# A mixture-of-experts layer: expert results added to the resident rows by transfers instead of by engines

## What is computed

```python
x = x + tanh(g_xattn) * xattn(layernorm(x), ctx, ...)        # 32 sequences of 64 rows
xf = layernorm(x)
probs = softmax(xf @ gate_w.T); top_p, top_i = top_k(probs, 2)        # 8 experts
y = sum over the two chosen experts e of
    p_e * (silu(xf @ fc1[e].T) * (xf @ fc2[e].T)) @ proj[e].T         # width 176
shared = silu(xf @ s1.T) * (xf @ s2.T) @ shared_proj.T                # width 704
y = y + sigmoid(xf @ shared_gate_w.T) * shared
x = x + tanh(g_ffn) * y
```

## Time and profile before

| | |
|---|---|
| median of 3 runs | 327.76 us (327.75 to 328.55) |
| the profiled execution | 328.36 us |
| its span | 326.6 us |
| mean granted TensorE clock | 0.969 |
| TensorE busy | 285.0 us, 87% |
| VectorE busy | 219.9 us, 67% |
| ScalarE busy | 170.6 us, 52% |
| GpSimd busy | 116.4 us, 36% |

### The profile page before, as it was taken

How to read it: one execution, slowest core, us unless ns; L and a number is a source line. 1 busy time by engine, 2 the same in 40 slices (tenths; PEclk the granted TensorE clock), 3 DMA queues, 4 the chain that set the end, 5 groups by cost and what they waited for, 6 DMA issues and landing times.

```text
span 326.6 us, 5834 instructions
## 1 busy us (share of the span) xinstructions
PE 285.0 (87%) x1783; PEld 252.2 (77%) x1783; DVE 219.9 (67%) x694; ACT 170.6 (52%) x399; POOL 116.4 (36%) x146
## 2 busy tenths in 40 slices
PE   0696979989998987797899999899999999999962
PEld 0565959878877765486788887789999999998852
DVE  3655766969868773666466764787777777743684
ACT  1537677777655454355023554456666666644220
POOL 0510351441773416641450000014444444441840
PEclk9999999999999998699799999999999999999985
DMA  6460114211044102533242565344666644314935
GB/s 225 171 194 0 67 49 130 64 48 66 36 135 163 51 19 99 189 136 101 107 151 65 198 206 188 113 134 137 202 203 202 201 139 135 109 67 138 350 125 193
DMA packets 25999, 43.32 MB, mean 133 GB/s; under 512 B 2961, under 2 KB 19601, under 8 KB 25969
## 3 DMA queue, kind: packets, MB, share of 16 engines
q1 hardware_dynamic: 22128, 33.20, 31.8%
q0 software_dynamic: 3408, 9.57, 8.1%
q10 hardware_dynamic: 432, 0.18, 0.3%
HBM read 26.35 MB, written 16.59 MB: 131 GB/s over the span
## 4 chain that ended last, share of the span: by engine, by line
PE 57%; DVE 20%; ACT 10%; issue 6%; DMA 4%; POOL 1%; SPq 0%; DVEq 0%; ACTq 0%; POOLq 0%
PE bank L416 43%; PE bank L639 8%; DVE ew_lo L961 4%; ACT ew_hi L741 4%; PE bank L716 3%; PE bank L681 2%; DVE work L1260 2%; DMA weight_stage<-wa_dram 2%; DVE xt_lo L961 2%; ACT sh_hi L741 2%; DVE neg_max L1001 2%; DMA weight_stage<-ew_dram 1%; ACT xn_all L778 1%; DVE sh_lo L961 1%; ACT work L773 1%
## 5 line engine op out<-in xcount | busy, mean ns | idle before, releaser
L1420 POOL DMA_INDIRECT y_d<-work,dest_of_slot x39 | 37.4, 959 | 88.4 <-ACT work L741 87.2
L416 PE MATMUL bank<-ew_hi,xt_hi 128*128 (+2 forms) x172 | 58.2, 339 | 0.3 <-issue 0.3
L416 PE MATMUL bank<-ew_lo,xt_hi 128*128 (+2 forms) x172 | 51.8, 301 | 0.0
L416 PE MATMUL bank<-ew_hi 128*128 128x256 f32 (+1 forms) x100 | 33.1, 331 | 15.8 <-ACT ew_hi L741 14.1
L961 DVE TENSOR_TENSOR xt_lo<-bank,xt_hi 128x256 fp32r<-128x256 f32 (+2 forms) x90 | 35.7, 398 | 11.6 <-ACT xt_hi L741 11.5
L416 PE MATMUL bank<-ew_hi,xt_lo 128*128 (+1 forms) x133 | 40.6, 305 | 0.0
L416 PE MATMUL bank<-xt_hi,sw_hi 128*128 128x512 f32 x88 | 36.1, 410 | 2.0 <-DVE work L1260 2.0
L741 ACT ACTIVATE xt_hi<-bank 128x256 fp32r<-128x256 f32 (+1 forms) x90 | 36.3, 409 | 2.8 <-PE bank L424 1.6
L416 PE MATMUL bank<-xt_lo,sw_hi 128*128 128x512 f32 x88 | 35.6, 405 | 0.0
L961 DVE TENSOR_TENSOR ew_lo<-bank,ew_hi 128x512 fp32r<-128x512 f32 (+1 forms) x41 | 22.7, 581 | 19.0 <-ACT ew_hi L741 18.9
L416 PE MATMUL bank<-xt_hi,sw_lo 128*128 128x512 f32 x88 | 35.3, 401 | 0.0
(11 more groups left out here) (157 smaller groups left out, 705.6 us busy)
## 6 DMA issues: line engine op xcount, KB each, us to landing
work<-xs_d SPq DMA_DIRECT2D x39, 136.0 KB, 2.5
weight_stage<-ew_dram SPq DMA_DIRECT2D x10, 486.5 KB, 4.2
ew_hi<-y_d SPq DMA_DIRECT2D x8, 512.0 KB, 7.9
xn_all<-x_dram SPq DMA_DIRECT2D x4, 512.0 KB, 5.0
work<-ctx_t_dram SPq DMA_DIRECT2D x4, 512.0 KB, 3.4
x_d<-work SPq DMA_DIRECT2D x4, 512.0 KB, 2.9
work<-x_d SPq DMA_DIRECT2D x3, 512.0 KB, 3.3
z_d<-work SPq DMA_DIRECT2D x3, 512.0 KB, 3.5
```

Source lines behind the costliest of these rows:

```text
L416: last = nc.tensor.matmul(dst, a, b, start=(n == 0), stop=(n == len(pairs) - 1))
L1420: nc.gpsimd.indirect_dma_start(out=y2_d, out_offset=bass.IndirectOffsetOnAxis(ap=IX[:, n:n + 1], axis=0), in_=EY[:, n % 4, :], in_offset=N ...
```

## The change

SyncE no longer loads the expert results, and the buffer `Y2`, GpSimd's four additions and VectorE's four (`combine`, with the semaphores `g_c1` and `v_c2`) are gone. GpSimd waits for the scatters and issues eight transfers of 512 KB from `y2_d` that add to `XNR`: first those of choice 0 for chunks 3, 0, 1, 2, each after the chunk's partial sums are loaded, then those of choice 1, each after the one of choice 0 for its chunk has landed. `s_sums(LAST)` and the stores wait for the transfers of choice 1.

```diff
@@ SyncE
-            sp.wait_ge(e_y, SLOT_TILES)
-            for r in range(4):
-                sp.wait_ge(d_ey[r], 16 * len(range(r, SLOT_TILES, 4)))
-            for c in LAST_FIRST:
-                for i in range(TOP):
-                    sp.dma_start(Y2[i][:, c * TPC:(c + 1) * TPC, :], y2_t[i, c]).then_inc(d_y[i][c], 16)
             for c in range(LAST - 1):
-                sp.wait_ge(v_c2, c + 2)
+                sp.wait_ge(d_y[1][c], 16)
                 sp.dma_start(out_c[c], XNR[:, c * TPC:(c + 1) * TPC, :]).then_inc(d_out, 16)
             for t in range(LAST * TPC, N_T):
                 sp.wait_ge(v_z, t + 1)
                 sp.dma_start(out_t[t], XNR[:, t, :]).then_inc(d_out, 16)
-            sp.wait_ge(v_c2, N_CH)
+            sp.wait_ge(d_y[1][LAST - 1], 16)
             sp.dma_start(out_c[LAST - 1], XNR[:, (LAST - 1) * TPC:LAST * TPC, :]).then_inc(d_out, 16)
@@ VectorE
-            def combine(n):
-                c = LAST_FIRST[n]
-                dve.wait_ge(g_c1, n + 1)
-                dve.wait_ge(d_y[1][c], 16)
-                t = slice(c * TPC, (c + 1) * TPC)
-                nc.vector.tensor_tensor(XNR[:, t, :], XNR[:, t, :], Y2[1][:, t, :], ALU.add).then_inc(v_c2, 1)
...
                 else:
-                    dve.wait_ge(v_c2, 1)
+                    dve.wait_ge(d_y[1][LAST], 16)
...
-                    if j >= 3:
-                        combine(j - 3)
             s_sums(LAST)
-            combine(3)
@@ GpSimd
-            for c in LAST_FIRST:
-                t = slice(c * TPC, (c + 1) * TPC)
-                pool.wait_ge(d_zl[c], 16)
-                pool.wait_ge(d_y[0][c], 16)
-                if PRE <= c < LAST:
-                    pool.wait_ge(v_z, 4 * c + 4)
-                nc.gpsimd.tensor_tensor(XNR[:, t, :], XNR[:, t, :], Y2[0][:, t, :], ALU.add).then_inc(g_c1, 1)
+            for r in range(4):
+                pool.wait_ge(d_ey[r], 16 * len(range(r, SLOT_TILES, 4)))
+            for i in range(TOP):
+                for c in LAST_FIRST:
+                    t = slice(c * TPC, (c + 1) * TPC)
+                    pool.wait_ge(*((d_zl[c], 16) if i == 0 else (d_y[0][c], 16)))
+                    nc.gpsimd.dma_start(XNR[:, t, :], y2_t[i, c], accum_op=ALU.add).then_inc(d_y[i][c], 16)
```

More of the change, by code:

```diff
@@ L183, in build @@
         EH = WK[:, 5536:6048].rearrange("p (r n) -> p r n", r=2)
-        Y2 = [EW[0][:, i * N_T * D:(i + 1) * N_T * D].bitcast(F32).rearrange("p (t n) -> p t n", n=D) for i in range(TOP)]
         XNR = XN[:, :, 0:D]
@@ L229, in build @@
         d_zl = [sem(f"d_zload{c}") for c in range(N_CH)]
-        g_pay, g_c1, e_ix = map(sem, ("g_payload", "g_c1", "e_ix"))
+        g_pay, e_ix = map(sem, ("g_payload", "e_ix"))
         zeroed, tanh_g, rw_hi, rw_lo = map(sem, ("zeroed", "tanh_g", "rw_hi", "rw_lo"))
@@ L256, in build @@
         e_xl, e_h, e_hl = map(sem, ("e_xl", "e_h", "e_hl"))
-        v_c2 = sem("v_c2")
         block = stack.enter_context(nc.Block())
```

## The result

The changed kernel takes 333.75 us (median of 4, 332.85 to 334.44) against 328.15 for the kernel before in the same comparison; the ratio of the two times is 1.0134 with a 95% interval of 1.0087 to 1.018 (the quotient of the two medians, 1.0171 or 5.6 us, lies within it). Run again beside two of the experiments it gave 1.0103 (1.0072 to 1.0135). By the two ratios it is slower by 1.0 to 1.3%, 3.4 to 4.4 us; the forecast was +5.2 us.

The account below looks back on a forecast made before the run. Computing of the last chunk, colliding with GpSimd's additions, was taken to end last; after the change eight adding transfers of 3.0 us would, hiding 5 us saved: +5.2 us on a median of 327.76 gives 333.0 us, range 324 to 344.

Parts of the forecast that it names:

- Computing gains 5 us: After the last block's fc: with GpSimd's and VectorE's additions gone, computing ends at 318.2 instead of 323.2.
- The gain is hidden: At the kernel's end: the DMA chain is the new end, with the 5 us saved in computing under it.
- The issue price: GpSimd issuing each adding transfer: between 1.26 and 4.14 us, taken as below 3 us, hidden except for the first.
- Start of the data: First adding transfer after the scatters land: data begins about 300.0, half a microsecond after the loads of before.
- My reading of the landing: Expert-result loads of the kernel before: first data passed by about 300.9, its semaphore arriving about 1.5 us later.
- Data, the largest term: Eight adding transfers in the DMA engines: two reads in turn, 3.0 us each, 24.0 us in all, on the path.
- The break-even of 2.4 us: Per adding transfer, in data and issue: below 2.4 us the change gains, above it loses.
- The stores: At the end: chunk 0's store between the last two additions, final store issued at 327.4, span ends at 331.8.
- The signs: From 300 on: DMA share high to about 325, some 175 GB/s, subtraction 0.69 us, SyncE's longest wait past 325.
- the dear issue: Rival on GpSimd's queue: descriptors written slower than engines use them, 4.14 us each, 337.3 by the median; chance 0.17.
- the three passes in turn: Rival in the DMA engines: two reads and a write in turn, 4.5 us each, 344.6 by the median; chance 0.13.
- the cheap addition: Rival in the DMA engines: an addition costs little more than a load, 1.5 us, 322.7 by the median; chance 0.15.

Follow-up runs that it names:

- the gate on GpSimd: Kernel before with VectorE's additions and SyncE's stores reordered, GpSimd's fourth addition held until VectorE's subtraction of block 4 is done; ratio 1.0001 (0.9961 to 1.004).
- the copies: Changed kernel with the eight transfers copying instead of adding; ratio to the kernel before 0.9872 on GpSimd's queue, 0.9887 on SyncE's queue.
- the hybrids: Changed kernel with half of the additions back on VectorE, fed by SyncE's loads, in two orders; ratios to the kernel before 1.0011 and 0.9995.

## Why the prediction was right

Slower was forecast with a chance of 0.80 by a mechanism that the runs confirm; the sum was +5.2 us and the span grew by 4.5 (331.1 against 331.8 forecast, with a last scatter that was itself 0.5 us later). That the two spans meet within 0.7 us is partly luck: the additions took 2.8 us less than forecast, and a late start of the data (1.6 us) and a slow end (1.5 us) took about as much more. Step by step:

- **Computing gains 5 us.** Forecast: sums end at 318.1 for a last scatter at 295.19. Found: 318.9 for 295.67. Right to 0.3 us; the ten last matmuls took 1.47 us and not 1.2. The subtraction's 2.79 us survive a change of VectorE's order and vanish with the gate on GpSimd: that the two engines' additions and subtractions hold each other up is shown.
- **The gain is hidden.** Shown by the kernel whose computing is 5 us later and whose tail isn't.
- **The issue price.** I took less than 3 us and hid it; it is 1.3 us. Right, near the low end.
- **Start of the data.** Forecast at 300.0. From 300 to 301 only 7 GB/s moved, and by 303 only 0.27 MB had, the work of 1.4 us at 198 GB/s; the rate was full from then on (192). In effect the data began at 301.6, 1.6 us late, 0.5 of it the late scatter. My reading of the landing was off as well: by finer stretches of the kernel before, the first load's 0.524 MB have passed at about 301.2 and not 300.9, so the addition at 302.36 came 1.2 us behind the data and not 1.5.
- **Data, the largest term.** Forecast 3.0 us each, 24.0 in all; found 2.65, 21.2 in all. This term was mis-sized by 0.35 us each. That the engines have no room for a second read fits, since twice 198 is 396 GB/s where the plain loads of the earlier trace rows read 348; but as said above, it is supported and not shown, and a part of the price goes with the small pieces. The break-even of 2.4 us lies below it, and the copies with their 1.5 us lie below that and were faster, so the point where the sign turns is bracketed by runs (additions in 4 KB pieces, about 2.5 us each, also had a longer tail than the kernel before).
- **The stores.** Here the step failed: I let chunk 0's store slip in between the last two adding transfers and counted only 1.0 us of stores ahead of the last one. In fact none was served before GpSimd's queue was nearly dry, at about 323; then all 2.1 MB of stores took some 5.5 us. The final store left at 325.76, 1.6 us earlier than forecast, but needed 331.1 - 325.76 = 5.3 us instead of 4.35. At its issue 1.1 MB of stores were left to move, its own half included, 3.0 us at 380 GB/s; 0.9 us pass behind the last byte, as before; the remaining 1.5 us are the slow end (23 GB/s from 329 to 331), which I hadn't foreseen and which no run explains. The order of the stores doesn't matter as long as the engines are full, as the kernel with the tile stores first shows. (A slip without effect: with chunk 0's store between the last two additions, chunk 1's would land at 322.5, not 324.0.)
- **The signs.** DMA share and subtraction came as said, the bytes moved at 195 and not 175 GB/s, and GpSimd issued its last transfer at 313.94. SyncE's longest wait wasn't the one that I named: it waited 39.0 us for the transfer of chunk 0, and only 0.4 us, to 325.76, for the last one, because the stores ahead of it were issued so late.

Of the rivals, the dear issue (4.14 us) and the three passes in turn (4.5 us) are excluded by the measured 1.3 and 2.65 us; the cheap addition is excluded by the difference of 8.1 us to the copies, 5.5 us of it at equal packets.

## What to carry to other kernels

An addition made by a transfer frees the engines but cost the DMA engines here 1.8 times a copy of the same bytes (about 1.7 times in pieces of 4 KB), so it pays only where they have room: before, they were full for 12 us in this stretch and had room afterwards (0.31 from 315 to 320 in the earlier trace rows); now they are full until the stores are out. Before trading work of an engine for work of the transfers, write down both ends, computing and transfers with the stores that follow, and see which will be last. And where several adding transfers go to the same rows, keep enough other rows in flight to hide the wait from one landing to the next, which the hybrids didn't do.

## What was not expected

- A plain store of SyncE gets nothing for 3 to 4 us while adding transfers of GpSimd's queue run (issued 319.73, first bytes after 322; issued 318.95, first bytes after 322), against 0.9 us on idle engines, and one issued in their midst took 8.9 us to land instead of 2.9. Behind copying transfers of that queue it was 1.7 us (311.36 to after 313), so it isn't the addition that keeps the store out.
- GpSimd needs 1.3 us to issue an adding transfer of 512 rows of 1 KB, 0.77 us (3.09 / 4) for the copy of the same rows, 0.92 us (3.66 / 4) for an adding transfer in 4 KB pieces, and 0.96 for a scatter of 128 rows. The copy also ran in 4 KB packets, so most of the dearer issue goes with the number of packets (512 for 128) and only some 0.15 us with the addition.
- The DMA share of adding transfers is 1.23 where that of loads at the engines' limit is 1.10: a share above one means that the times of packets overlap, and in 4 KB pieces additions moved more bytes (203 GB/s) at a share of 1.03. So the share alone doesn't say how many bytes an engine can still take.
